# A mixed-decay block on one core: the two parts of rwkv allocated ahead of the scans' buffer

## The reference

```python
xm = xn * time_mix + shifted(xn) * (1 - time_mix)       # xn = layernorm(x)
k  = exp(minimum(xm @ Wk.T, 60)); v = xm @ Wv.T; r = xm @ Wr.T
wkv   = decayed_sum_over_time(k * v)                    # per head, first token weighted apart
sum_k = decayed_sum_over_time(k) + 1e-16
rwkv  = sigmoid(r) * wkv / sum_k
attn  = rwkv @ Wo.T
ffn   = clip(layernorm(xn) * 128 / gamma) @ ternary(weight) * (gamma * beta / 128)
out   = x + attn + ffn                                  # gamma: the largest absolute value of all
```

## Time and profile before

| | |
|---|---|
| runs, median of 3 | 896.96 us (896.64 to 898.52) |
| profiled execution, span from first to last instruction | 894.1 us |
| profiled execution, outside the span | not recorded; 2.9 us if it took the median |
| PE busy | 870.5 us, 97% |
| VectorE busy | 765.6 us, 86% |
| ScalarE busy | 510.8 us, 57% |
| GpSimd busy | 214.9 us, 24% |

### The profile page before, as it was taken

How to read it: one execution, slowest core, us unless ns; L and a number is a source line. 1 busy time by engine, 2 the same in 40 slices (tenths; PEclk the granted TensorE clock), 3 DMA queues, 4 the chain that set the end, 5 groups by cost and what they waited for, 6 DMA issues and landing times.

```text
span 894.1 us, 12792 instructions
## 1 busy us (share of the span) xinstructions
PE 870.5 (97%) x3984; PEld 713.4 (80%) x3984; DVE 765.6 (86%) x1278; ACT 510.8 (57%) x834; POOL 214.9 (24%) x242
## 2 busy tenths in 40 slices
PE   3889999999999999999999999999999999999998
PEld 2778888888888888888888888888888888888886
DVE  5998999989898999989997897878978788789684
ACT  5584757667594757576563554535545536365441
POOL 5453326152442425240030110200201103011000
PEclk9999999999999999999999999999999999999999
DMA  7322415051423224054642245314452443424311
GB/s 282 111 79 99 137 63 173 12 173 51 164 70 135 100 93 142 12 176 135 207 155 104 83 153 188 129 71 140 152 175 58 154 141 101 149 92 141 95 48 47
DMA packets 59841, 107.13 MB, mean 120 GB/s; under 512 B 7712, under 2 KB 7712, under 8 KB 59808
## 3 DMA queue, kind: packets, MB, share of 16 engines
q1 hardware_dynamic: 59808, 106.73, 35.2%
HBM read 64.76 MB, written 41.96 MB: 119 GB/s over the span
## 4 chain that ended last, share of the span: by engine, by line
PE 90%; DVE 4%; issue 2%; POOL 2%; ACT 1%; DMA 0%; SPq 0%; DVEq 0%; POOLq 0%; ACTq 0%
PE kvr L514 18%; PE kvr L512 18%; PE kvr L513 17%; PE out_banks L533 7%; PE out_banks L532 7%; PE out_banks L530 7%; PE out_banks L553 6%; PE out_banks L551 6%; PE transposed L465 2%; PE out_banks L465 2%; DVE bn_stats L841 2%; POOL normed L1173 1%; POOL own_stats L1155 1%; POOL own_stats L1156 1%; DVE wv_lo L926 0%
## 5 line engine op out<-in xcount | busy, mean ns | idle before, releaser
L1246 POOL TENSOR_TENSOR evacuated<-normed,mix_over_ffn_row 128x512 f32<-128x512 f32 x28 | 51.3, 1831 | 339.0 <-DVE ffn_lo L921 339.0
L512 PE MATMUL kvr<-xm_hi,wv_hi 128*128 128x512 f32 x256 | 102.8, 401 | 3.6 <-DVE wv_lo L926 2.6
L512 PE MATMUL kvr<-xm_hi,wk_hi 128*128 128x512 f32 x256 | 103.3, 403 | 2.6 <-DVE xm_lo L921 2.6
L512 PE MATMUL kvr<-xm_hi,wr_hi 128*128 128x512 f32 x256 | 102.8, 402 | 0.0
L530 PE MATMUL out_banks<-wo_hi,rwkv_hi 128*128 128x512 f32 x256 | 101.5, 397 | 0.0
L533 PE MATMUL out_banks<-wo_hi,rwkv_lo 128*128 128x512 f32 x256 | 101.2, 395 | 0.0
L532 PE MATMUL out_banks<-wo_lo,rwkv_hi 128*128 128x512 f32 x256 | 101.2, 395 | 0.0
L514 PE MATMUL kvr<-xm_hi,wk_lo 128*128 128x512 f32 x256 | 100.6, 393 | 0.0
L514 PE MATMUL kvr<-xm_hi,wr_lo 128*128 128x512 f32 x256 | 100.2, 391 | 0.0
L513 PE MATMUL kvr<-xm_lo,wk_hi 128*128 128x512 f32 x256 | 100.2, 391 | 0.0
L514 PE MATMUL kvr<-xm_hi,wv_lo 128*128 128x512 f32 x256 | 100.1, 391 | 0.0
(11 more groups left out here) (140 smaller groups left out, 1934.9 us busy)
## 6 DMA issues: line engine op xcount, KB each, us to landing
other<-ffn_input SPq DMA_DIRECT2D x64, 256.0 KB, 5.4
x<-in_x SPq DMA_DIRECT2D x15, 1024.0 KB, 5.7
other<-in_x SPq DMA_DIRECT2D x8, 1024.0 KB, 5.8
ffn_input<-evacuated SPq DMA_DIRECT2D x32, 256.0 KB, 4.7
ffn_input<-parked SPq DMA_DIRECT2D x32, 256.0 KB, 2.2
attn_scratch<-x SPq DMA_DIRECT2D x8, 1024.0 KB, 4.4
parked<-attn_scratch SPq DMA_DIRECT2D x8, 1024.0 KB, 7.1
out<-parked SPq DMA_DIRECT2D x8, 1024.0 KB, 5.2
```

What stands on the lines that cost most here:

```text
L512: nc.tensor.matmul(KVR[:, m, :], hi, XH[t][:, ch, :], start=(ch == 0), stop=False)
L1246: G.tensor_tensor(U[:, n % RING, :], XN[:, ch, :], BC[:, :], ALU.mult).then_inc(pool_v, 1)
```

## The change

The buffer of the scans is allocated behind the two parts of rwkv instead of ahead of them. So `rwkv_hi` and `rwkv_lo` begin at multiples of 128 bytes, where they began 32 bytes over a multiple of 64. `scans` begins 16,384 bytes higher. The three together end where they ended, and all other tensors keep their addresses. No instruction changes but for these addresses.

```diff
         E = sb("gate", [P, 2, TILE])
-        S = sb("scans", [P, 2, TILE + 1])
         RH = sb("rwkv_hi", [P, CH, TILE], F32R)
         RL = sb("rwkv_lo", [P, CH, TILE], F32R)
+        S = sb("scans", [P, 2, TILE + 1])
 
         BC = sb("mix_over_ffn_row", [P, TILE])
```

## The result

The changed kernel takes 892.0 us (median; 891.33 to 893.7), the kernel before 897.29 in the same comparison (896.42 to 899.33). The ratio is 0.9942, with a 95% interval of 0.9929 to 0.9955: faster by 4.0 to 6.4 us. The profiled execution took 892.2 us, with a span of 890.4.

A forecast was written before the change was run, and what follows sets the result against it. PE, busy 97% of the span, was taken to bound the kernel. The projection's 768 matmuls would save 4.9 us, all else 0: 896.96 - 4.9 = 892.1 us, range 890.8 to 895.0.

The forecast's parts named there:

- The bound: Whole kernel: PE, busy 97% of the span, sets the end; a nanosecond on each matmul is paid in full.
- The 2.9 us outside the span: Around the profiled span: the runs' median 896.96 less the span 894.1 leaves 2.9 us, taken to stay.
- The size of the term: Output projection: 768 matmuls drop from 233.1 to 226.6 ns pitch, 5.0 us, or 4.8 against 226.9; 4.9 taken.
- the lower bound: Projections of phase A come down only to 229.1 ns, giving 1.5 us; with phase B's 2.5, 4.0 us together.
- bounds of 4.0 and 5.0: Projection's gain in us: 4.0 if phase A reaches only 229.1 ns, at most 5.0; times 892.0 to 893.0.
- The rival by which only phase B gains: Projections of phase A stay at 233.1 ns because loads lag behind transposes; gain 2.5 us, time 894.5; chance 0.07.
- The step that failed: Projection: rwkv_hi and rwkv_lo, loaded 32 bytes over a multiple of 64, cause the excess; 6.5 ns per matmul.
- the place is not the cause, or nothing changes: Projection: the loaded operand's place costs nothing, gain 0 us, time 897.0; chance 0.14.
- the three readings that I ruled out: Projection's slow pitch: not the PSUM bank change, not the weights' high, high, low order, not a wait; no size given.
- Writers and scans: ScalarE and VectorE writes of rwkv_hi and rwkv_lo, and scans at the moved buffer: durations unchanged, 0 us each.
- The margin of 0.31 us: Phase A, first projection's fourth chunk: rwkv_lo is ready 0.31 us before its load; the gain takes 0.23, leaving 0.08.
- What I assumed of the mechanism: Projection's weight loads: load rows stay 188 ns, the load takes something from the stream beside it; 6.5 ns per matmul.

The follow-up runs named there:

- the run with Wo off: The changed kernel with wo_hi and wo_lo, which stream in the projection, allocated behind the scans' buffer (distance 480); 898.81 us in one execution.
- the run with the scans ahead at distance 0: The kernel before, scans' buffer still ahead, small tensors and padding bringing rwkv_hi and rwkv_lo to distance 0 modulo 512 from wo; 892.11 us, ratio 0.9949.

## Why the prediction was right, and where its reasoning was not

*The bound.* Right. PE sets the end, and a nanosecond on each of 768 matmuls was paid in full: the projections gave 4.7 us by start times, and from PE's first matmul to the end it was 4.6. That the median met 892.1 to 0.1 us is chance: the executions of the changed kernel alone spread by 2.4 us, and the medians are 5.3 us apart. The 2.9 us outside the span were too many: 892.2 - 890.4 leaves 1.8, and the executions of the kernel before that have both numbers leave 1.8 or 1.9. The term stands on both sides of the sum and drops out.

*The size of the term.* Right in the main: the pitch fell from 233.1 to 226.7 in phase B, and in half of phase A. The other half, behind transposes, came down to 229.6 alone, as the lower bound had it for all of phase A, but from 234.8. So phase A gave 2.2 us, and the sum is 4.7 where 4.9 was forecast, inside its bounds of 4.0 and 5.0. The rival by which only phase B gains was right that the pitch behind transposes is raised whatever the place, and wrong that nothing is gained there.

*The step that failed* is the one that names the cause: "What remains in the code is where the operand that is loaded as weights lies." The premise stood in the text two sentences on: the streamed operand lies at a multiple of 128 in all three products. That left two readings, the loaded operand's place and its distance from the streamed one, and the trace of before cannot tell them apart, since every fast product has both the place and the distance. I took the first without a word on the second. The runs showed the second: a multiple of 64 or 128 at another distance gains next to nothing (233.3 and 232.5 ns), a place 32 over at distance 0 gains it (227.3), and moving the streamed operand alone loses it (233.5). The number was right because the change sets both at once, which for the cause was luck.

*The rival "the place is not the cause, or nothing changes".* Its first half was true, and its second was not; I had tied them together. Among the three readings that I ruled out (banks, order of the weights, a wait) the distance was missing. As for the page that spoke for it (the Trainium skill, SBUF — State Buffer, Specifications (TRN2)): lines of 16 bytes would make 32, 64 and 128 alike, and alike they are. But the rule has no term for a second operand.

*Writers and scans.* Right: 630 and 686 ns for the writers, 1226, 1286 and 1303 for the scans and L982.

*The margin of 0.31 us.* Right in that PE got no new kind of wait. In the first batch `rwkv_lo` now ends at 76.64 us and the load starts at 76.81:

```profile
75.95 0.69 DVE L995 TENSOR_TENSOR rwkv_lo<-k_and_kv,rwkv_hi 128x512 fp32r<-128x512 f32 x1 [0.70 <-ACT rwkv_hi L749]
...
76.81 0.19 PEld L530 LDWEIGHTS out_banks<-wo_hi,rwkv_hi 128*128 128x128 f32 x1
```

0.17 us are left of 0.31; I had expected 0.08.

*What I assumed of the mechanism,* that a load takes something from the stream beside it, is neither shown nor ruled out: the dearest matmul is the one that streams while the load that is off comes in, and at distance 0 13.3 ns stand over the stream for each matmul with its load, whether 512 or 256 columns stream. The Trainium skill, TensorE: Matmul & The Clock Gate, Part 2: What happens when you issue a matmul, gives the array two independent read ports, one for the stream and one for the weight load. By that no distance could matter; some 19 us for 32 bytes of padding say that here the two do depend on each other. Where they meet, and why 233 ns at 512 columns turns into less than 120 at 256, was not shown here.

## What to carry to other kernels

Look at the distance between the operand that a matmul loads and the one that streams beside it, not at the place of one of them: here 0 modulo 512 bytes was the fastest found with 512 columns, with 256 as fast, and one odd-sized buffer allocated ahead of a matmul operand cost 6.5 ns on every matmul that loads it. Put buffers of odd sizes last, and read the pitch from start times in a stretch without waits; the duration of the load does not show it, and the mean duration of the matmul shows it only as 397 or 395 ns beside 389. And when a change sets two things at once, a right number proves neither: move them apart, each by itself.

## What the runs showed of the hardware

- The pitch of a 128x512 matmul with its own load, at 2.4 GHz and in fp32r, was 226.7 ns at distance 0 in phase B, and 232.5 to 235.0 at 32, 64, 96, 128, 224, 352, 416 and 480; at 256 it was 226.7 in the group shown, and up to 231.2 in groups behind a product of another distance, in which the first eight or nine matmuls were 224 to 236 ns apart. With 256 columns it was 120.0 at distance 0 and 118.3 at 32.
- Executions of one kernel differed by some 2 us with the mean granted clock: of the changed kernel those at 1.000 took 891.33 to 892.2 us, those at 0.992 and 0.994 893.68 and 893.7. Of the kernel before, in the comparisons of the experiments, 21 executions at 1.000 took 896.4 us in the mean and 17 at 0.992 or 0.994 took 898.3, with some overlap. The loss lies in the start. In the run with Wo off (0.994) the clock was 0.72 of full speed from 18 to 22 us, behind PE's first waits, where the run with the scans ahead at distance 0 (1.000) had 1.00; from 60 us on both had 1.00. One row of each, in that order (stretch, length, busy time of PE, PEld, DVE, ACT and POOL, clock, DMA share, GB/s):

```profile
18.00:22.00 4.00, 3.01 (x7) 1.82 (x8) 4.00 (x10) 1.88 (x4) 3.63 (x6) 0.72 0.51 193
```
```profile
18.00:22.00 4.00, 3.92 (x8) 2.42 (x9) 4.00 (x10) 2.23 (x4) 3.24 (x5) 1.00 0.51 186
```

A mean of 0.72 is that of a stretch in which PE ran partly at 1.2 GHz, partly at 2.4. The pitches above are taken behind the start, at a granted clock of 1.00.
